# Causal masks of the attention scores: from TensorE's matmuls to VectorE's row maxima and GpSimd's clears

## The reference

```python
x = x + latent_attention(layernorm(x)) + experts(layernorm(x))         # top 4 of 8 experts
xn = layernorm(x)
x = x + sparsemax_attention(xn) + grouped_attention_then_experts(xn)   # 4 key heads, top 2 of 8
# each attention, 16 heads of 16 features, 512 x 512 scores per head:
scores = where(causal, q @ k.T * scale, -large)
attn = softmax(scores)        # latent ("mla") and grouped ("gqa")
attn = sparsemax(scores)      # the third one ("spm")
ctx = attn @ v
```

## Time and profile before

| | |
|---|---|
| runs | 3161.73, 3164.6, 3172.23 us, median 3164.6 |
| profiled execution | its span, first to last instruction, is 3156.2 us; the page gives no other time for it |
| granted TensorE clock, mean | 0.960 |
| PE busy | 2801.0 us (89%) |
| DVE busy | 2182.1 us (69%) |
| ACT busy | 1613.7 us (51%) |
| POOL busy | 1508.6 us (48%) |

### The profile page before, as it was taken

How to read it: one execution, slowest core, us unless ns; L and a number is a source line. 1 busy time by engine, 2 the same in 40 slices (tenths; PEclk the granted TensorE clock), 3 DMA queues, 4 the chain that set the end, 5 groups by cost and what they waited for, 6 DMA issues and landing times. The chain is left out here.

```text
span 3156.2 us, 60542 instructions
## 1 busy us (share of the span) xinstructions
PE 2801.0 (89%) x20990; PEld 2273.0 (72%) x20990; DVE 2182.1 (69%) x6269; ACT 1613.7 (51%) x3388; POOL 1508.6 (48%) x2213
## 2 busy tenths in 40 slices
PE   3878789999999999978898889898799999999996
PEld 2555478889888888846666666666588888888864
DVE  4788778777777777757777777767645455454576
ACT  1545344444454444445655566565455555555554
POOL 3587853443343344375556666322233333332487
PEclk8878799999999999989999999999899999999998
DMA  2464668778778778622334444210356666565445
GB/s 82 175 224 172 229 244 304 279 284 298 281 284 291 285 271 295 244 39 53 96 93 107 108 108 108 92 67 23 136 192 223 219 210 233 202 231 207 139 96 126
DMA packets 192066, 580.08 MB, mean 184 GB/s; under 512 B 22856, under 2 KB 144656, under 8 KB 157456
## 3 DMA queue, kind: packets, MB, share of 16 engines
q1 hardware_dynamic: 154896, 525.03, 46.2%
q0 software_dynamic: 36864, 51.14, 8.0%
HBM read 450.14 MB, written 125.96 MB: 183 GB/s over the span
## 5 line engine op out<-in xcount | busy, mean ns | idle before, releaser
L542 PE MATMUL bank<-xh,gu 128*128 128x256 f32 x3520 | 677.1, 293 | 49.6 <-DMA gu<-wu_scratch 28.8
L1160 POOL TENSOR_TENSOR al<-t,ah 128x512 fp32r<-128x512 f32 x220 | 283.5, 1289 | 879.7 <-ACT ah L1394 879.7
L542 PEld LDWEIGHTS bank<-xh,gu 128*128 128x128 f32 x3520 | 515.8, 191 | 78.0 <-DMA gu<-wu_scratch 34.9
L1491 ACT ACTIVATE pt<-bank 128x512 f32<-128x512 f32 (+1 forms) x1152 | 510.8, 542 | 53.2 <-PE bank L606 50.5
L1851 DVE TENSOR_REDUCE st<-bank 128x1 f32<-128x512 f32 (+3 forms) x1024 | 422.0, 481 | 155.5 <-PE bank L603 149.9
L585 PE MATMUL bank<-masks_bf,ident_bf 128*128 128x128 bf16 x1896 | 430.7, 251 | 104.7 <-DVE st L1851 39.7
L603 PE MATMUL bank<-ksT,qsT 128*128 128x512 f32 (+3 forms) x1536 | 409.1, 367 | 5.6 <-DVE top L1849 3.1
L1499 ACT ACTIVATE oT<-bank 128x512 f32<-128x512 f32 x192 | 114.6, 597 | 577.9 <-PE bank L682 577.8
L585 PEld LDWEIGHTS bank<-masks_bf,ident_bf 128*128 128x128 bf16 x1896 | 169.6, 98 | 314.2 <-DVE st L1851 100.3
L606 PE MATMUL bank<-qaT,ksT 128*128 128x512 f32 (+3 forms) x1536 | 390.1, 370 | 0.0
L542 PE MATMUL bank<-xl,gu 128*128 128x256 f32 x1760 | 353.3, 282 | 0.0
(11 more groups left out here) (254 smaller groups left out, 5246.7 us busy)
## 6 DMA issues: line engine op xcount, KB each, us to landing
gu<-wu_scratch SPq DMA_DIRECT2D x110, 2056.0 KB, 8.2
dn<-wd_scratch SPq DMA_DIRECT2D x110, 1024.0 KB, 10.4
xs<-xs_scratch SPq DMA_DIRECT2D x110, 264.0 KB, 2.7
ys_scratch<-yb SPq DMA_DIRECT2D x110, 256.0 KB, 10.7
raw<-in_gu SPq DMA_DIRECT2D x16, 1024.0 KB, 6.7
wu_scratch<-hi SPq DMA_DIRECT2D x16, 1024.0 KB, 10.0
wu_scratch<-lo SPq DMA_DIRECT2D x16, 1024.0 KB, 13.7
xs_scratch<-empty SPq DMA_DIRECT2D x32, 264.0 KB, 6.2
```

What stands on the lines that cost most here:

```text
L542: mm = pe.matmul(bank[:, TS * h:TS * (h + 1)], gu[:, col:col + P], x[s % 2][:, TS * k:TS * (k + 1)], start=(n == 0), stop=(n == len(terms) ...
L1160: pool.tensor_tensor(em["al"][s % 2][:, m, :], em["t"][g % 2][:, :], em["ah"][s % 2][:, m, :].bitcast(F32), ALU.subtract).then_inc(al_read ...
L1491: act.activation(to, frm, ACT.Relu if kind == "spm" else ACT.Exp).then_inc(s_act, 1)
```

## The change

The mask of the queries' scores of the softmax layers (mla and gqa) is no longer a matmul. A bf16 tile `causal`, 0 in its first 384 columns and the triangular mask in its last 128, is added by VectorE in the same instruction that takes the row's extreme: `tensor_tensor_reduce` adds scores and mask, multiplies by -1, writes the result over the scores in PSUM, and gives the minimum of it as accumulator output, which is the negated maximum that line 1867 made before. That line goes. Sparsemax queries keep their masks.

The keys' units lose their mask in all steps from 21 to 176 outside the grouped layer, so in 24 more steps (50 to 63 and 128 to 137); in these `clear(G, 0)` and `clear(G, 1)` are put at the end of GpSimd's step, and `outputs(G)` waits for them.

```diff
+    causal = sb("causal", [P, T], BF16)
...
+                dve.memset(causal[:, 0:T - P], 0.0).then_inc(filled, 1)
...
+                dve.tensor_copy(causal[:, T - P:T], masks[:, 0, :]).then_inc(cast, 1)
-                dve.wait_ge(cast, 2)
-                dve.wait_ge(filled, 5 + len(fills))
+                dve.wait_ge(cast, 3)
+                dve.wait_ge(filled, 6 + len(fills))
...
+        bare_pairs = [G for G in range(begins[0], ends_at[1]) if kinds[G // NP] != "gqa"] if em else []
...
-                    bare = which == "k" and G in plan
-                    masks_last = which == "q" and len(S.banks) == len(units)
+                    sparse_rows = kinds[G // NP] == "spm"
+                    bare = G in bare_pairs if which == "k" else not sparse_rows
+                    masks_last = which == "q" and sparse_rows and len(S.banks) == len(units)
...
-                    if G in plan:
-                        pe.wait_ge(pt_ready, 4 * (1 + sorted(plan).index(G)))
+                    if G in bare_pairs:
+                        pe.wait_ge(pt_ready, 4 * (1 + bare_pairs.index(G)))
...
+                    if G in bare_pairs and G not in plan:
+                        clear(G, 0)
+                        clear(G, 1)
...
-                                ins = dve.reduce_max(st[:, 0, r:r + 1], bank[:, first:first + width], AX.X)
+                                scored = bank[:, first:first + width]
+                                ins = dve.tensor_tensor_reduce(scored, scored, causal[:, T - width:T], -1.0, -MASKED,
+                                                               ALU.add, ALU.min, st[:, 1, r:r + 1])
...
-                    if not spm:
-                        chain(dve.tensor_scalar(st[:, 1, :], st[:, 0, :], -1.0, None, ALU.mult))
-                    else:
+                    if spm:
```

## The result

The changed kernel takes 3199.4 us (median of 4 runs, 3194.99 to 3200.81), the kernel before on the same chip 3164.2: a ratio of 1.0108, 95% interval 1.0091 to 1.0125, so 35 us slower. The profiled execution has a span of 3193.4 us, 37.2 above before's 3156.2. The sum forecast +33.4, but some of its terms missed in opposite directions.

A forecast was written before the change was run, and what follows sets the result against it. VectorE's maxima, not TensorE, were taken to close the query-score bursts. Terms +21.3, -2.7, +9.6, +2.7 and +2.5 gave +33.4 us on the 3156.2 us span; with 8.4 carried over for the runs' median, 3198 us, range 3150 to 3240.

The forecast's parts named there:

- VectorE closes the burst of query scores; the masks are worth nothing there: Grouped steps: TensorE's last score unit waits for three VectorE maxima, so removing six masks a step is worth 0.
- 3d: Ordinary softmax steps: three maxima precede the last unit's release, each costing d = 0.09 us more, all added to the step.
- d = 0.09: VectorE's softmax-query maxima: each costs 0.09 us more than now, for the accumulator read; bounds 0 and 0.21.
- The grouped term: Grouped layer, eight sequences: VectorE's extra load at borders and 3d in six other steps each, +21.3 us.
- Steps 21 to 49, -2.7: First experts' steps: 11.6 us of masks saved, less 3.9 for weights and 5.0 for VectorE's load.
- I give a third back: Steps 21 to 49: of 11.6 us of masks saved, 3.9 is lost again to waits for experts' weights.
- Steps 50 to 63, +9.6: These steps: late clears on GpSimd cost 7.4 us, and eight quiet steps paying 3d cost 2.2.
- Steps 128 to 137, +2.5: These steps: the clear of step 135 stands behind eight scatters and delays its outputs; +2.5 us, bounds 0 to 3.1.
- Steps 0 to 20, +2.7: First steps: a quarter of VectorE's 10.9 us extra load counts, as GpSimd's scatters hold the steps as often.
- The first rival (d = 0): Softmax-query maxima: no second instruction, so no extra cost per maximum; 3161 us, no change to be told, chance 0.20.
- the long read: Softmax-query maxima: the next instruction waits for the accumulator read's end, 0.21 us per maximum; 3248 us, chance 0.14.
- TensorE as the bound: Query bursts: TensorE sets their length, so removed masks make the kernel faster, 3115 us; chance 0.12.

## Why the prediction was right, and where it was not

*VectorE closes the burst of query scores; the masks are worth nothing there.* Shown, from both sides: masks out with nothing in their place gain nothing (651.8 for 650.2), an earlier release with all masks kept gains 12. But it is not the whole mechanism. The prediction gave VectorE's whole load to the borders alone and 3d to the other six steps of a sequence. One of these six is filled by VectorE as a border is and paid 0.21, not 0.15.

*d = 0.09.* Mis-sized: 0.05. A second record came each time (1024 in all), but the next main instruction starts with the read, where ScalarE's started 0.09 behind it, and the 0.05 may be the two-input operation's own. The grouped term with d = 0.05 is 10.4 where the sum had 21.3; measured 12.8, and 11.5 for the operation with masks kept.

*Steps 21 to 49, -2.7.* +0.6 in the changed kernel, -1.1 with the operation there alone, -0.8 with no price at all: nothing that can be told from the scatter of this stage. The step that failed is "I give a third back": of 14.9 us less TensorE work 13.4 came back as waits for weights, gc and yb.

*Steps 50 to 63, +9.6.* 16.1. Taken apart: keys 12.3 (predicted 7.4), queries 4.0 (2.2). The clears' own price was right, 1.44 us for four in the row above. Wrong was that the loss starts with the clear of step 51 and ends with `outputs(53)`. GpSimd's queue is full in steps 51 to 55, so every clear from step 50 on pushes what stands behind it: the stack of step 54, which the prediction had 4.4 late, came 6.6 late, and that of step 56 10.3. The prediction kept this case as its upper bound of 12. Keeping the masks in just these steps gave the keys' part back within 1 us.

*Steps 128 to 137, +2.5.* 4.9. `outputs(135)` waits 7.8 us for pt, as foretold, and its clear costs about 2, near the term. Without it 3.7 stay. Of these, 1.9 are in step 130, where the granted clock is 0.88 in place of 1.00, which the prediction had no term for; why it falls there, and the other 1.8, stay open.

*Steps 0 to 20, +2.7.* 2.2. On the other chips this stage scatters more than the term, so it is not tested further.

The total came out within 2 us by luck: the grouped layer's 8.5 us too much and the 12 too little in steps 50 to 63, 128 to 137 and the experts' stage cancel in the main, to 3.8 too little on the span; and the runs' median lies 6.0 above the profiled span, not the 8.4 carried over, which hides 2.4 of them. The first rival (d = 0) fell with the records, the long read with the pitch, TensorE as the bound with the masks left out. The query part and the key part cost 1.0087 and 1.0059 alone; together on the first chip 1.0108, less than their product, 1.0147. Why they don't add up isn't settled; other chips and the scatter of steps 0 to 20 are in it.

## What to carry to other kernels

Taking work from the busiest engine gains nothing where its bursts end on another's release; first ask whose semaphore the last unit of the burst waits for, and bring that release forward (here by reordering units, one line) before moving work onto the engine that gives it. Ask it step by step: in a step that the other engine fills from end to end its whole load counts, and an earlier release gains nothing. A piece of work handed to an in-order queue costs by what stands behind it in the stretch where that queue is full, so look at the fullest steps, not at the mean share. If an extra result can come out of an instruction that is there anyway (the negated maximum from the plain reduce), take it from there.

## What the runs showed of the hardware that was not expected

The accumulator read of VectorE takes 0.14 us in its record, yet a back-to-back maximum with it takes only 0.05 us more than a plain one. The granted clock of the grouped layer was 0.97 to 0.98 in each profile with TensorE's query masks and 0.94 to 0.96 in each without; its price in time was not separable there. In step 130 it was: 12.90 us at a granted clock of 1.00, 14.6 to 14.8 at 0.88, with the same waits of TensorE to within 0.3 us. The same kernel takes 346 us for steps 0 to 20 on one chip and 375 on another, with the later stages within some 4 us; the DMA rate there is 194 against 181 GB/s, and whether that is cause or effect stays open.
